# 48 instead of 32 batches multiplied by the weight while x is first read, in a graph-layer kernel on one core

## What is computed

```python
h = jnp.maximum(_layernorm(x, axis=-1), 0.0)
# the layer of the graph; xp is h with the nodes in front: (n, batch, t)
x_avg = xp.mean(axis=1)
x_norm = x_avg / jnp.maximum(norm(x_avg), 1e-12)
sim = (x_norm @ x_norm.T + 1.0) * 0.5
adj = (sim + gumbel[:, 0] > 1.0 - sim + gumbel[:, 1])
adj_sym = clip(adj + adj.T, 0, 1); nmask = clip(adj_sym + eye, 0, 1)
common = nmask @ nmask.T
W = adj * where(valid, common / common.max() * common, 0.0)
Wn = dinv[:, None] * W * dinv[None, :]
xw = jnp.einsum('nbt,to->nbo', xp, weight)
out = jnp.einsum('sd,sbt->dbt', Wn, xw) + bias
result = x + transpose(out)
```

## Time and profile before

| | |
|---|---|
| median of 3 runs | 922.95 us (921.21 to 923.11) |
| the profiled execution's own time | 921.26 us |
| its span in the trace | 919.5 us |
| TensorE busy, granted clock | 887.7 us (97%), 0.999 |
| VectorE, ScalarE, GpSimd busy | 725.3, 328.0, 239.8 us |
| moved by the DMA engines | 160.25 MB, mean 174 GB/s |
| until the last sum over batches starts (L824) | 123.2 us |

### The profile page before, as it was taken

The page is one execution under the profiler, slowest core; times in us unless marked ns, Lnnn a source line. Parts: engine busy times, 40 slices in busy tenths (PEclk is TensorE's granted clock), DMA queues, the critical chain, the costliest instruction groups (busy, mean ns, idle before and its releaser), DMA issues.

```text
span 919.5 us, 12305 instructions
## 1 busy us (share of the span) xinstructions
PE 887.7 (97%) x4563; PEld 761.4 (83%) x4567; DVE 725.3 (79%) x1471; ACT 328.0 (36%) x531; POOL 239.8 (26%) x188
## 2 busy tenths in 40 slices
PE   4999999999999999999999999999999999999997
PEld 3777665788788888888888888888889888988886
DVE  7878858899989797888879787868576758677687
ACT  4999935651221121302121211323333342424130
POOL 4799960500212121111111111302011111111111
PEclk9999999999999999999999999999999999999999
DMA  9999889233436170716344352615233252524122
GB/s 355 382 419 381 328 326 422 81 123 116 137 138 206 69 275 6 269 61 214 105 170 140 135 190 85 225 50 198 77 134 141 90 185 69 183 92 161 46 92 92
DMA packets 37484, 160.25 MB, mean 174 GB/s; under 512 B 3376, under 2 KB 3504, under 8 KB 32176
## 3 DMA queue, kind: packets, MB, share of 16 engines
q1 hardware_dynamic: 37424, 159.46, 46.8%
HBM read 108.07 MB, written 51.38 MB: 173 GB/s over the span
## 4 chain that ended last, share of the span: by engine, by line
PE 79%; DVE 9%; ACT 6%; POOL 3%; issue 2%; DMA 0%; DVEq 0%; ACTq 0%; POOLq 0%
PE ps L1354 69%; PE ps L1303 4%; ACT main L532 4%; DVE bmem L957 3%; POOL main L473 3%; ACT bmem L541 2%; PE ps L1224 2%; DVE stats L750 2%; PE ps L1206 1%; DVE bmem L950 1%; PE ps L1137 1%; PE ps L1284 1%; DVE main L1070 1%; DVE main L1046 1%; DVE bmem L969 0%
## 5 line engine op out<-in xcount | busy, mean ns | idle before, releaser
L1354 PE MATMUL ps<-bmem,main 128*128 128x256 f32 x3136 | 685.1, 379 | 4.0 <-DVE main L1037 2.6
L1354 PEld LDWEIGHTS ps<-bmem,main 128*128 128x128 f32 x3136 | 592.4, 190 | 83.3 <-DVE main L1037 3.5
L500 POOL TENSOR_TENSOR main<-main 128x256 f32<-128x256 f32 x32 | 28.7, 896 | 477.3 <-ACT main L659 424.0
L1037 DVE TENSOR_TENSOR main<-ps,main 128x512 f32<-128x512 f32 x124 | 76.5, 623 | 71.0 <-PE ps L1354 71.0
L490 POOL TENSOR_TENSOR main<-main 128x256 f32<-128x256 f32 (+1 forms) x96 | 91.9, 984 | 139.0 <-DVE main L1030 139.0
L1046 DVE TENSOR_TENSOR main<-main 128x256 f32<-128x256 f32 (+1 forms) x256 | 124.5, 558 | 0.0
L473 POOL TENSOR_TENSOR main<-main 128x1024 f32<-128x1024 f32 x41 | 96.9, 2364 | 23.4 <-ACT main L532 18.5
L619 ACT ACTIVATE ps<-ps 128x512 f32<-128x512 f32 x64 | 33.8, 528 | 159.2 <-PE ps L1354 159.2
L750 DVE BATCH_NORM_STATS2 stats<-main 128x6 f32<-128x512 f32 x128 | 81.2, 674 | 4.5 <-DMA main<-in_x 4.5
L877 DVE TENSOR_TENSOR main<-main 128x256 f32<-128x256 f32 x112 | 48.2, 431 | 44.7 <-PE ps L1354 41.5
L1137 PEld LDWEIGHTS ps<-w_sb,main 128*128 128x128 f32 x560 | 67.0, 194 | 15.0 <-issue 12.0
(11 more groups left out here) (101 smaller groups left out, 541.2 us busy)
## 6 DMA issues: line engine op xcount, KB each, us to landing
main<-in_x SPq DMA_DIRECT2D x92, 512.0 KB, 7.2
main<-in_x SPq DMA_DIRECT2D x32, 1024.0 KB, 6.7
out<-main SPq DMA_DIRECT2D x31, 1024.0 KB, 4.9
main<-spill SPq DMA_DIRECT2D x17, 1024.0 KB, 5.3
spill<-bmem SPq DMA_DIRECT2D x16, 1024.0 KB, 11.9
main<-in_L_gnn_gumbel SPq DMA_DIRECT2D x8, 1024.0 KB, 6.3
spill<-main SPq DMA_DIRECT2D x2, 512.0 KB, 4.6
out<-main SPq DMA_DIRECT2D x1, 512.0 KB, 4.9
```

The lines of the kernel that those rows point to most:

```text
L1037: dve.tensor_tensor(at, piece(slot, b), at, ALU.add).then_inc(s, 1)
L1354: last = pe.matmul(piece(slot, b)[:, QUARTER * e:QUARTER * (e + 1)], left_[:, blk(c)], right_[:, c, :], start=slot in FRESH and b < 3 and ...
```

## The change

The list of spilled pairs grows from 16 to 24, so 48 batches are multiplied by the weight in stage 1. `LOADED` becomes quads 2 to 13, and `WEIGHED` becomes quad 1 and quads 14 and 15. Twelve spills instead of four stand between reads, and the 24 places in `bmem` are all used twice. GpSimd sums both batches in 16 pairs instead of 9. VectorE copies four more of the products; `BY_VECTOR` names their pairs and the group and step of the statistics behind which each stands. Around quads 0 and 1 some instructions of VectorE and TensorE change order. TensorE starts the transposes one comparison earlier and starts the slots 0, 2 and 6 of quad 0 with the parts that need no inner sums.

```diff
-    SPILLED = [0, 1, 2, 3, 5, 7, 8, 9, 11, 13, 15, 17, 19, 21, 23, 26]
-    AHEAD = [4, 6]
+    SPILLED = [0, 1, 2, 3, 4, 5, 7, 9, 10, 11, 12, 13, 14, 15, 16, 17, 19, 20, 21, 22, 23, 24, 25, 26]
+    AHEAD = [6, 8]
-    SPILLED_EARLY = [15, 17, 19, 21]
-    HOMES = [*range(8, 16), *range(16, 24), *range(8), *range(8, 16)]
+    SPILLED_EARLY = [16, 17, 18, 19, 21, 22, 23, 25, 26, 27, 28, 29]
+    HOMES = [*range(8, 24), *range(8), *range(8, 24), *range(8)]
+    BY_VECTOR = {5: (7, 0), 9: (8, 2), 11: (9, 4), 21: (14, 3)}
+    LAG = (2, 3)
+    MADE = [product(q, b) for p in range(PAIRS) for q, b in ((p - 1, 1), (p, 0)) if q in SPILLED]
+    VECTOR_COPIES = [*(product(p, 1) for p in BY_VECTOR), KEPT - 2, KEPT - 1]
...
-    BOTH = [4, 6, 8, 11, 14, 16, 18, 20, 23]
+    BOTH = [4, 5, 6, 7, 9, 12, 13, 14, 15, 16, 17, 19, 22, 23, 25, 27]
...
             def spill_group(g):
-                if g == KEPT // 2 - 1:
-                    sp.wait_ge(s_kept_last, 2)
-                else:
-                    sp.wait_ge(s_kept, 2 * g + 2)
+                wait_copied(sp, 2 * g)
+                wait_copied(sp, 2 * g + 1)
...
+            def keep(p, b):
+                n = product(p, b)
+                wait_made(dve, n)
+                if HOMES[n] in HOMES[0:n]:
+                    dve.wait_ge(s_spill[HOMES.index(HOMES[n]) // 2], 16)
+                dve.tensor_copy(kept[:, HOMES[n], :], bank(2 + 2 * b, 2)).then_inc(s_kept_vector, 1)
...
-                    finish_kept(quad - 1, 0, u_keep, s_g21, 16 * quad - 8)
                 else:
                     prepare(3)
-                if quad:
+                if quad == 1:
+                    inner_sums(quad, 3)
+                    finish_kept(0, 0, u_keep, s_g21, 0)
+                    finish_kept(0, 1, v_keep, s_g22, 8)
+                elif quad:
+                    finish_kept(quad - 1, 0, u_keep, s_g21, 16 * quad - 8)
                     inner_sums(quad, 3)
...
                 if quad == 0:
+                    add_kept(quad, 4, v_keep, s_vkeep, s_g22)
                     prepare(6)
...
-                    add_kept(quad, 6, u_keep, s_ukeep, s_g21, range(2))
-                finish_kept(quad, 1, v_keep, s_g22, 16 * quad + (0 if quad + 1 < QUADS else 8))
-                if quad:
-                    finish(quad, 1)
+                    add_kept(quad, 6, u_keep, s_ukeep, s_g21, range(1))
+                else:
+                    finish_kept(quad, 1, v_keep, s_g22, 16 * quad + (0 if quad + 1 < QUADS else 8))
+                finish(quad, 1)
...
-            pe.wait_ge(s_adj, C)
+            pe.wait_ge(s_adj, C - 1)
...
+            for i in range(2):
+                for j in range(C - 1):
+                    transpose(i, j)
+            pe.wait_ge(s_adj, C)
+            for i in range(2):
+                transpose(i, C - 1).then_inc(s_tr, 1)
...
-            pe.wait_ge(s_repc, 2)
...
+                    if quad == 0 and slot in (0, 2, 6):
+
+                        if slot == 0:
+                            pe.wait_ge(s_comb, 4 * n + 4)
+                            pe.wait_ge(s_scaled, KC)
+                            pe.wait_ge(s_repc, 1)
+                            times(0, 0, 2, 0, q[0, 1], moving[1, 0])
+                            times(0, 0, 2, 1, s4, moving[1, 1])
+                            free(0, 0, 0)
+                            times(0, 0, 0, 0, q[0, 0], moving[0, 0])
+                            pe.wait_ge(s_repc, 2)
```

More of the change, by code:

```diff
@@ L528, in relu @@
                 if p - HPAIRS in SPILLED:
-                    act.wait_ge(s_hw, 2 * SPILLED.index(p - HPAIRS) + 2)
+                    wait_made(act, product(p - HPAIRS, 1))
                 for b in range(2):
@@ L548, in _ @@
                         std(t + 1)
-                    if p - 3 in SPILLED[:-1]:
-                        keep(p - 3, 1)
-                    if p - 2 in SPILLED[:-1]:
-                        keep(p - 2, 0)
+                    for b in (1, 0):
+                        q = p - LAG[b]
+                        if q in SPILLED and product(q, b) in SCALAR_COPIES:
+                            keep(q, b)
             for f in range(2):
@@ L678, in _ @@
                 for b in range(4):
-                    keep_bank(quad, 2, b, u_keep, 16 * quad, s_ukeep)
+                    keep_bank(quad, 2, b, u_keep, 8 if quad == 1 else 16 * quad, s_ukeep)
                     weigh(quad, (2, b))
                 for b in range(4):
-                    keep_bank(quad, 3, b, v_keep, 16 * quad - 8, s_vkeep)
+                    keep_bank(quad, 3, b, v_keep, 16 if quad == 1 else 16 * quad - 8, s_vkeep)
                     weigh(quad, (3, b))
@@ L768, in _ @@
                     for b in range(2):
-                        n = KEPT - 2 + b
-                        dve.wait_ge(s_hw, n + 1)
-                        dve.wait_ge(s_spill[HOMES.index(HOMES[n]) // 2], 16)
-                        dve.tensor_copy(kept[:, HOMES[n], :], bank(2 + 2 * b, 2)).then_inc(s_kept_last, 1)
+                        keep(SPILLED[-1], b)
                     whole_chain(t)
                 else:
-                    for c, between in enumerate((aggregate, invert, quotient, newton, set_rstd, set_shift)):
-                        long_step(t, c)
-                        if t > 3:
-                            between(t - 1)
-                    long_step(t, 6)
-                    long_step(t, 7).then_inc(s_bn, 1)
+                    stages = (aggregate, invert, quotient, newton, set_rstd, set_shift)
+                    for c in range(steps):
+                        last = long_step(t, c)
+                        if c == steps - 1:
+                            last.then_inc(s_bn, 1)
+                        if t > 3 and c < len(stages):
+                            stages[c](t - 1)
+                        for p, at in BY_VECTOR.items():
+                            if at == (t, c):
+                                keep(p, 1)
             chain = [0]
@@ L1113, in _ @@
                     finish_kept(quad, 0, u_keep, s_ukeep, 16 * quad)
-                add_kept(quad, 4, v_keep, s_vkeep, s_g22)
+                if quad:
+                    add_kept(quad, 4, v_keep, s_vkeep, s_g22)
                 if quad + 1 < QUADS:
@@ L1152, in keep_product @@
             def keep_product(p, b):
-                n = 2 * SPILLED.index(p) + b
-                wait(pe, s_kept, n - 1)
+                n = product(p, b)
+                if n >= 2:
+                    wait_copied(pe, n - 2)
                 times_weight(h1[:, p % HPAIRS, b, :], 2 + 2 * b).then_inc(s_hw, 1)
```

73 lines of the change are left out of this document (46 added, 27 removed).

## The result

| | before | the change |
|---|---|---|
| median | 923.0 us | 910.82 us |
| lowest to highest of 4 runs | 921.21 to 923.11 | 908.48 to 911.81 |
| ratio, with its 95% interval | | 0.9871 [0.9857, 0.9885] |
| the profiled execution, its span | 921.26, 919.5 us | 911.81, 910.1 us |
| TensorE busy, granted clock | 887.7 us (97%), 0.999 | 877.6 us (96%), 0.996 |

The change is 12.2 us faster by the medians, where 16.5 were predicted. The profiled pair is 9.4 us apart. The executions of before fall into two levels, near 921.4 us with a mean granted clock of 0.998 or 0.999 and near 923.0 us with 0.997; the profiled one is of the lower level and the median of the upper, while the profile of the change is of its slowest execution.

A forecast was written before the change was run, and what follows sets the result against it. Prediction: GpSimd ends stage 1, VectorE is full from 187.5 to 242.6 us, TensorE from there on; -28.5 + 15.2 + 0.5 - 0.4 - 3.3 = -16.5 us, so 922.95 - 16.5 = 906.4 us, range 901 to 915.

The forecast's parts named there:

- Stage 3, -28.5 us: Stage 3: 32 half batches less between the products with the graph, at 0.89 us each, all on the path: -28.5 us.
- Rival 4: Stage 3: quads 9 to 13 don't get shorter with VectorE at 84%, giving 935 us; chance 0.03 together with rival 3.
- GpSimd, +15.2 us: Stage 1: 44 additions left from 27.48 us on, at 2.50 us each plus 0.8 of gaps, end at 138.4: +15.2 us.
- Stage 2 and quads 0 and 1, -3.7 us: Transposes start one comparison earlier, -0.4 us; TensorE's waits around quad 0 shrink, -3.3 us.
- rival 5: Stage 2 gives nothing: 910 us, within the range and counted in the forecast's chance of 0.70.
- that start at 254 to 256: Sign in the profile: TensorE's steady products, which started at 242.6 us before, start at 254 to 256.
- Spills and `gumbel`, +0.5 us: End of stage 1: `gumbel` loads behind four spills land about at the sum's end or 1 to 2 us later: +0.5 us.
- TensorE's cover: Stage 1: TensorE's last sum comes between 131 and 137 us, covered by GpSimd's later end by 1 to 7 us.
- The reads: Stage 1: at 420 GB/s the last read lands at 113 us, 11 us in hand, so the added spills cost nothing.
- rival 1: The reads bound stage 1: at 351 GB/s it ends at 147 instead of 138.4, giving 915 us; chance 0.15.
- rival 3: Copies, spills, reads and ReLUs wait in a loop from a 33 us landing on; slower than before; 0.03 together with Rival 4.

The follow-up runs named there:

- e9: The kernel before with only the changed list `BOTH` (48 GpSimd additions, seven TensorE sums less): 938.67 us, ratio 1.0174.
- e7: e6 with eight of quad 1's sixteen additions moved behind the inner sums for slot 4: 919.18 us, ratio 0.9959.
- e6: The change's new instruction order around quads 0 and 1, with the tables of the kernel before: 922.0 us, ratio 0.9997.
- e2: The change with the first two loads of `gumbel` ahead of the last of the four spills in SyncE's queue: 909.0 us, ratio 0.986.
- e0: The change run again unaltered, on the chip of e1 to e3: 910.57 us, 0.9871 of the kernel before.
- e3: The change with pair 14 out of `BOTH`, so GpSimd makes 47 additions and TensorE one more batch sum: 910.33 us, ratio 0.9866.
- e5: The change with e1's move, three `gumbel` loads ahead of the last spill and e3's 47 additions: 904.58 us, ratio 0.981.
- e8: e5 with each of the twelve early spills writing only the first of its two products, a measurement leaving data out: 902.65 us, ratio 0.9785.
- e1: The change with eight of quad 1's sixteen additions moved behind the inner sums for slot 4: 905.72 us, ratio 0.9823.
- e4: The change with the moves of both e1 and e2: 904.49 us, ratio 0.9806.
- e10: e11 with the list `BOTH` of the kernel before, so GpSimd makes 41 additions: 910.3 us, ratio 0.9868.
- e11: The change with e1's move and three loads of `gumbel` ahead of the last spill, 48 additions kept: 904.85 us, ratio 0.9808.

## Why the prediction was right, and what was wrong in its size

The direction and the range (901 to 915) hold. The likeliest value, 906.4, is 4.4 us too low.

- **Stage 3, -28.5 us: right.** 2288 instructions in a row, no wait in quads 9 to 13, `weigh` x192 as forecast, and the 28.5 us are found between the last two lines of the balance once the clock is added. Rival 4 (quads no shorter) fell.
- **GpSimd, +15.2 us: right.** 15.35 in the change, 15.0 at the sum in e9, which does this part alone. Its floor of 44 additions held, with 0.6 us of gap for the 0.8 taken and a start 0.4 us later (27.84). Two side sums are off without bearing on it: 27.48 + 37 x 2.50 + 3.5 is 123.5 and not 123.3, and a last read at 113 with 13 us behind it leaves 12 us to 138.4 and not 11.
- **Stage 2 and quads 0 and 1, -3.7 us: this step failed.** I had written that the eight additions "come later in quad 1, where VectorE has about 1 us of room before TensorE wants slot 1's place in PSUM", and put nothing down for it. But eight additions take 3.5 us, and the room was 0.5 us where 1 had been read, less what TensorE gained in quad 0 itself. The gains in quad 0 came in the size walked through, and e7 shows them, with stage 2's, as 3.6 us. One remainder stands at another place: 0.62 us at slot 1, where 0.7 had been put at slot 4. 2.5 us of the gains went into the new wait, and in the change another 1.6 into TensorE's clock. That is why the order alone (e6) gave 0.8 us. It is nearly rival 5, with its 910, which had been held to be part of the forecast. Of the signs, "that start at 254 to 256" failed here: the last wait ends at 273.83.
- **Spills and `gumbel`, +0.5 us of a range of 0 to 3: too low.** The loads landed late enough that the second comparison ran at 143.90, 5.3 us behind the reading of the sum; VectorE waited 2.8 us, and the scaling of the mean stands behind these comparisons on VectorE. The load that it waited for took some 10 us from issue to landing (from 133.69 on, in the change's chain of waits), where the prediction had counted 2.5 us for each transfer in the queue. Removing it is worth 1.6 us (e2).
- **TensorE's cover "by 1 to 7 us", its last sum "at 134": there was none.** Its last sum ended at 138.2 (137.3 in e0), beyond the late side of the band of 131 to 137. None of the idleness was used up: TensorE's products waited 6.1 us for copies and its sums 12.9 for ReLUs, 4.1 and 13.4 before. And the sum was not the last thing: two late products of 3.57 us stand between it and the column sums. Before they ran beside GpSimd's last additions, and the prediction costed them at nothing without a word on their cover. By itself this cost at most 0.3 us (e2). But TensorE and GpSimd now bind together, and moving work from GpSimd to TensorE brings nothing (e3, e5).
- **The reads "cost nothing": nearly.** VectorE's 14.8 us of waiting is over the 10 us that I had named as the sign for rival 1, but most of it has cover. With half the early spills 1.9 us are won (e8), not the 9 of rival 1. The rate that decides it was 414 to 424 GB/s in the windows of 5 us from 60 to 115 us, near the 420 that I had taken from the row of before.
- **The loop of places in `bmem` (rival 3): did not close.** A spill landed after 25.3 us at most, where 33 would have begun to count. The median of 8.7 us that I had read from the earlier trace rows holds loads too; the writes alone had 11.9, and 16.2 in the change.

The measured terms, each from the run that isolates it where there is one: -28.5 (stage 3), +15.0 (the sum, e9), +0.3 (late products, e2), +1.6 (`gumbel`, e2), -3.6 (the order, e7), +4.9 (the wait with its clock, e1) make -10.3 us. Taken from 921.26, the profiled execution of before, that is 911.0, and e0 measures 910.57. With the 4.4 us that the profiles of e0 and e1 show for the last term it is 910.5. The sum goes over terms from several runs, each good to some tenths of a us, so it doesn't tell the two apart. The medians are 12.2 apart because that of before lies 1.6 us above its profiled execution. These 1.6 us go with the lower mean clock, 0.997, of the executions at that level; where in the kernel it falls isn't known, as no profile of one was taken.

The version that beats both kernels is e4, the change with the additions and two loads moved: 904.5 us, 0.9806 of before. The sum of the prediction had put the profiled execution of the change there (904.8), but that is in part chance: e4 also has the loads of `gumbel` moved, and with the room in quad 1 alone (e1) it is 905.7.

## What to carry to other kernels

When work is moved off an engine's urgent place, look at what stands behind its new place: eight additions of 0.44 us put beside eight others, ahead of one zeroing of 0.27 us, took back most of what the new order had won, and moving them behind the zeroing gave it back. When the engine that ends a stage is given more work, list for every other engine what still stands in its queue between its last instruction of the stage and the first of the next; what was hidden by the old bound isn't hidden any more. And when two engines end a stage within 2 us of each other, taking work from one and giving it to the other measures as nothing.

## What the runs showed of the hardware

- **A short wait in a full stretch can cost more than itself.** In the profiles of the change, e0, e2 and e3 TensorE idled 2.49 or 2.50 us in quad 1, and the clock was then 0.66 to 0.92 in one or two windows of 5 us. In e9 it was 0.66 around waits of 2.97 and 3.00 us, and 0.68 behind one of 1.68 us before 139.61; in the change 0.70 around 1.97 us ahead of 106.54. But behind the 2.50 us of e6 and the 3.01 us of e9 at 123.23 no window was below 1.00. In e1, e4, e5, e7, e10 and e11 no window between 15 and 300 us is below 0.97. So it depends on more than the length of a wait. At this place the fall cost 1.6 us on top of the wait of 2.5. The Trainium skill (TensorE: Matmul & The Clock Gate, Why this matters for your kernels) tells of such falls after idleness, and the trace agrees in so far as each of these stood behind a wait.
- **Reads with writes between them moved as fast as reads.** Reads alone moved 415 to 420 GB/s in the windows of 5 us from 10 to 35 us of before; with spills among them the change shows 414 to 424 from 60 to 115 us.
- **Landing times under load are wide.** A write of 1 MB to `spill` took 16.2 us from issue to landing in the median and 25.3 at most in the change, and 11.9 and 23.1 before.
